# Q and K as three fp32r products each, narrower probability transposes, and a convolution loop written out

## What is computed

```
# convolution block: 1x1 (128 -> 64), 3x3 in 32 groups, 1x1 (64 -> 128), each with batch norm
h = relu(bn(conv(x, w1)));  h = relu(bn(conv(h, w2, groups=32)));  x = relu(bn(conv(h, w3)) + x)
# attention block, windows of 7 x 7, rolled by 3, 8 heads of 16 channels
y = layernorm(x) * norm1_w + norm1_b
q, k, v = split(windows(roll(y)) @ qkv_w.T)
attn = softmax(q @ k.T * 16**-0.5 + bias + mask)
x = x + unroll((attn @ v) @ proj_w.T + proj_b)
z = layernorm(x) * norm2_w + norm2_b
out = x + gelu(z @ fc1_w.T + fc1_b) @ fc2_w.T + fc2_b
```

## Time and profile before

| | |
|---|---|
| time, median of 3 runs | 4525.73 us (4525.11 to 4525.87) |
| time of the profiled execution | 4518.32 us |
| its span, first to last instruction | 4516.2 us |
| busy share of the span: PE, DVE, ACT, POOL | 98%, 70%, 76%, 49% |
| matmul instructions | 71190 |

### The profile page before, as it was taken

The page is one execution under the profiler, slowest core; times in us unless marked ns, Lnnn a source line. Parts: engine busy times, 40 slices in busy tenths (PEclk is TensorE's granted clock), DMA queues, the critical chain, the costliest instruction groups (busy, mean ns, idle before and its releaser), DMA issues.

```text
span 4516.2 us, 192181 instructions
## 1 busy us (share of the span) xinstructions
PE 4423.1 (98%) x71190; PEld 3178.5 (70%) x71190; DVE 3178.4 (70%) x7717; ACT 3415.4 (76%) x5644; POOL 2207.9 (49%) x3242
## 2 busy tenths in 40 slices
PE   8999996999999999999999999999999999999998
PEld 5666665677777777777777777777777777777775
DVE  4444444777777777777777777777777777777775
ACT  3444443888888888888888888888888888888886
POOL 4444442455554545455555555455555545455553
PEclk9999998999999999999999999999999999999999
DMA  4545442011111111111111111111111111111110
GB/s 138 153 151 163 151 153 66 25 30 29 29 29 30 30 29 29 29 30 29 29 29 30 30 29 29 29 30 29 29 29 29 29 29 29 30 30 29 29 29 26
DMA packets 298330, 218.64 MB, mean 48 GB/s; under 512 B 43377, under 2 KB 245518, under 8 KB 298190
## 3 DMA queue, kind: packets, MB, share of 16 engines
q1 hardware_dynamic: 294632, 215.41, 16.4%
q10 hardware_dynamic: 3558, 1.07, 0.1%
HBM read 110.73 MB, written 111.94 MB: 49 GB/s over the span
## 4 chain that ended last, share of the span: by engine, by line
PE 97%; DVE 1%; issue 1%; ACT 0%; POOL 0%; DMA 0%; DVEq 0%; POOLq 0%; ACTq 0%
PE bank L666 16%; PE bank L608 10%; PE bank L585 8%; PE bank L509 6%; PE bank L576 6%; PE bank L641 6%; PE bank L657 6%; PE bank L595 6%; PE bank L567 5%; PE bank L620 5%; PE bank L522 5%; PE bank L631 4%; PE bank L659 4%; PE bank L658 4%; PE bank L673 2%; PE bank L487 2%
## 5 line engine op out<-in xcount | busy, mean ns | idle before, releaser
L1234 POOL TENSOR_TENSOR sc<-sc,mx 128x784 f32<-128x784 f32 x512 | 779.2, 1522 | 940.9 <-DVE mx L1068 940.9
L666 PE MATMUL bank<-g,fc_sb 128*128 128x392 f32 x2048 | 785.4, 506 | 0.1
L1221 POOL TENSOR_TENSOR res<-x,projb 98x512 f32<-98x512 f32 x256 | 326.3, 1275 | 804.2 <-DVE x L1104 804.2
L861 ACT ACTIVATE g<-bank,fc1b 128x392 f32<-128x392 f32 x1024 | 560.6, 592 | 172.6 <-PE bank L659 172.6
L1087 DVE SCALAR_TENSOR_TENSOR xn<-x,lnp 98x128 f32<-98x128 f32 x1024 | 292.8, 349 | 491.1 <-POOL lnp L1157 491.1
L608 PEld LDWEIGHTS bank<-ident_sb,sc 128*113 128x113 f32 x4096 | 495.6, 177 | 113.1 <-DVE shared L1038 109.8
L666 PEld LDWEIGHTS bank<-g,fc_sb 128*128 128x128 f32 x2048 | 348.7, 190 | 306.2 <-issue 163.1
L608 PE MATMUL bank<-ident_sb,sc 128*113 128x128 f32 x4096 | 547.8, 277 | 0.1
L1062 DVE TENSOR_TENSOR sc<-bank,shared 128x392 f32<-128x392 f32 x1024 | 528.7, 560 | 2.8 <-PE bank L595 2.8
L1068 DVE TENSOR_REDUCE mx<-sc 128x16 f32<-128x784 f32 x512 | 496.6, 970 | 18.5
L1157 POOL TENSOR_TENSOR lnp<-lnp,half 98x8 f32<-98x8 f32 x518 | 467.7, 924 | 20.3
(11 more groups left out here) (105 smaller groups left out, 8258.3 us busy)
## 6 DMA issues: line engine op xcount, KB each, us to landing
x<-x_scratch SPq DMA_DIRECT2D x768, 49.0 KB
out_x<-y SPq DMA_DIRECT2D x672, 49.0 KB
xc_even<-in_x SPq DMA_DIRECT2D x128, 196.0 KB
shared<-in_x SPq DMA_DIRECT2D x128, 196.0 KB
x_scratch<-xc_even SPq DMA_DIRECT2D x128, 196.0 KB
x_scratch<-shared SPq DMA_DIRECT2D x128, 196.0 KB
x<-x_scratch SPq DMA_DIRECT2D x256, 38.5 KB
out_x<-y SPq DMA_DIRECT2D x224, 38.5 KB
```

The costliest lines, as they stand in the source:

```text
L666: mm = nc.tensor.matmul(RC[:, 0:ST], fc2[:, c, :], g[:, c], start=c == 0, stop=c == HC - 1)
L861: nc.scalar.activation(g[:, j], ring[:, 0:ST], ACT.Gelu, bias=fc1b[:, j:j + 1]).then_inc(out_, 1)
L1234: P.tensor_tensor(out=s_r, in0=s_r, in1=m_r.to_broadcast([128, 2 * HEADS, N]), op=ALU.subtract).then_inc(sub_done, 1)
```

## The change

1. Q and K are each computed by three fp32r products, with weights `wqk_hi`, `wqk_lo` (made once, on DVE) and input `xt_hi`, `xt_lo`. `xt_hi` is made in every strip by POOL (`xt_round`: xt times one, written as fp32r), `xt_lo` by DVE (`xt_rest`: xt minus xt_hi). Values still use xt in fp32.
2. Q goes to bank 0, one of the score banks, instead of `RA`; K and Q have separate semaphores, and `RA` has two jobs a strip from the projection instead of three.
3. PE's round begins with the values, then the transposes of z, then K and Q. ACT's begins with `v_out`, `zt_out`, `k_out`, and takes `gelu` 0 and 1 ahead of the first two `pt_out`.
4. The probability transposes take 113 rows of the scores and the identity cut to 113 x 113, instead of 128 rows and 128 x 128.
5. The loop over the convolution's pairs is written out: 16 calls of `period`.
6. PE starts the convolution's first step before the last preparations of weights on DVE are done.

```diff
@@ over_pairs
-    with e.Fori(0, (BPAIRS - 2) // 2) as k:
-        period(2 * k, 0)
-        period(2 * k + 1, 1)
-    period(BPAIRS - 2, 0)
-    period(BPAIRS - 1, 1)
+    for gp in range(BPAIRS):
+        period(gp, gp % 2)
@@ PE
-                pe.wait_ge(prep, len(PREP))
+                at(pe, "fc1_scaled")
...
+            def split_product(dst, part):
+                cols = slice(C * part, C * part + C)
+                nc.tensor.matmul(dst, wqk_hi[:, cols], xt_hi[:], start=True, stop=False)
+                nc.tensor.matmul(dst, wqk_lo[:, cols], xt_hi[:], start=False, stop=False)
+                return nc.tensor.matmul(dst, wqk_hi[:, cols], xt_lo[:], start=False, stop=True)
+
+            def project_k(t):
+                pe.wait_ge(a_out, A_JOBS * t.n + 1)
+                pe.wait_ge(xt_split, t.n + 1)
+                split_product(RA[:, 0:ST], 1).then_inc(a_full, 1)
+
+            def project_q(t):
+                wait(pe, s_out, QUADS * t.n)
+                split_product(bank[0][:, 0:ST], 0).then_inc(q_full, 1)
...
-                    mm = nc.tensor.transpose(RB[j % 2][0:VT, 128 * q:128 * q + 128],
-                                             sc[:, t.u, q, j].rearrange("p h m -> p (h m)")[:, 0:VT], ident[:])
+                    mm = nc.tensor.transpose(RB[j % 2][0:VT, 128 * q:128 * q + VT],
+                                             sc[0:VT, t.u, q, j].rearrange("p h m -> p (h m)")[:, 0:VT],
+                                             ident[0:VT, 0:VT])
@@ PE, strips
-                    project(t, 0)
                     values(t, 0)
                     values(t, 1)
...
-                    project(t, 1)
+                    project_k(t)
+                    project_q(t)
@@ ACT, strips
-                    k_out(t)
                     v_out(t)
...
+                    k_out(t)
...
+                    gelu(t3, 0)
+                    gelu(t3, 1)
                 if t1.there():
                     pt_out(t1, 0)
                     pt_out(t1, 1)
                 if t3.there():
-                    gelu(t3, 0)
-                    gelu(t3, 1)
@@ DVE
+            def xt_rest(t):
+                dve.wait_ge(xt_rounded, t.n + 1)
+                V.tensor_tensor(out=xt_lo[:], in0=xt[:].rearrange("c w n -> c (w n)"), in1=xt_hi[:].bitcast(fp32),
+                                op=ALU.subtract).then_inc(xt_split, 1)
@@ DVE, strips
                     y_sum(t3)
+                if ahead.there():
+                    xt_rest(ahead)
                 if t1.there():
                     x2_out(t1)
@@ POOL
+            def xt_round(t):
+                pool.wait_ge(a_out, A_JOBS * t.n + 1)
+                wait(pool, q_full, t.n)
+                x_ = xt[:].rearrange("c w n -> c (w n)")
+                tt(xt_hi[:], x_, one[:].to_broadcast([C, ST]), ALU.mult).then_inc(xt_rounded, 1)
@@ POOL, strips
                     subtract(t)
+                if ahead.there():
+                    xt_round(ahead)
```

More of the change, by code:

```diff
@@ L141 @@
              "sign", "scaled", "exponent", "power", "signed", "tab", "tab_ps", "tab_rows", "hidden_ps", "hidden", "table_ps", "table",
-             "fc1b_ps", "fc1b", "fc1_scaled", "fc1_hi", "fc1_lo"]
+             "fc1b_ps", "fc1b", "fc1_scaled", "fc1_hi", "fc1_lo", "wqk_hi", "wqk_lo"]
 PREP = CONV_PREP + BIAS_PREP
@@ L185, in program @@
         fc1_hi, fc1_lo = [sb(f"fc1_{i}", [C, HID], fp32r) for i in ("hi", "lo")]
+        wqk_hi, wqk_lo = [sb(f"wqk_{i}", [C, 2 * C], fp32r) for i in ("hi", "lo")]
         fc2 = sb("fc2_sb", [128, HC, C])
         half = sb("half", [128, C])
+        one = sb("one", [128, 1])
         quarter = sb("quarter", [PT, 2, PAIRS])
@@ L221, in program @@
         xt = sb("xt", [C, WINS, N])
+        xt_hi, xt_lo = [sb(f"xt_{i}", [C, ST], fp32r) for i in ("hi", "lo")]
         qt = sb("qt", [C, WINS, QROWS])
@@ L241, in program @@
         RA, RB, RC = bank[4], bank[5:7], bank[7]
-        A_JOBS = 3
+        A_JOBS = 2
         SUMS, PROJECTION = 2, 3
@@ L255, in program @@
         zt_split = sem("zt_split")
+        xt_rounded, xt_split, q_full, q_sb = sem("xt_rounded"), sem("xt_split"), sem("q_full"), sem("q_sb")
         conv2_begun, vb_clear = sem("conv2_begun"), sem("vb_clear")
@@ L579, in values @@
                     mm.then_inc(b_full[0], 1)
[L581 to L586, removed]
+            def split_product(dst, part):
[4 more added lines that the diff above has]
+            def project_k(t):
+                pe.wait_ge(a_out, A_JOBS * t.n + 1)
+                pe.wait_ge(xt_split, t.n + 1)
[3 more added lines that the diff above has]
+                split_product(bank[0][:, 0:ST], 0).then_inc(q_full, 1)
             def scores(t, i):
-                pe.wait_ge(a_out, A_JOBS * t.n + 3)
+                pe.wait_ge(a_out, A_JOBS * t.n + 2)
+                pe.wait_ge(q_sb, t.n + 1)
                 wait(pe, s_out, QUADS * t.n)
@@ L893, in strips @@
                     zt_out(t3)
+                if t.there():
+                    k_out(t)
                 if t3.there():
                     nc.scalar.preload_act_table_set("gelu_and_others")
+                if t3.there():
+                    gelu(t3, 0)
+                    gelu(t3, 1)
                 if t1.there():
@@ L970, in bias_steps @@
                          op=ALU.subtract)
+                    step("wqk_hi", V.tensor_copy, wqk_hi[:], wqkv[:, 0:2 * C])
+                    step("wqk_lo", V.tensor_tensor, out=wqk_lo[:], in0=wqkv[:, 0:2 * C], in1=wqk_hi[:].bitcast(fp32),
+                         op=ALU.subtract)
             def xct_out(gp, i):
@@ L1041, in q_out @@
             def q_out(t):
-                dve.wait_ge(a_full, A_JOBS * t.n + 3)
+                dve.wait_ge(q_full, t.n + 1)
                 wait(dve, s_full, t.n)
-                V.tensor_copy(qt[:, :, 0:N], RA[:, 0:ST].rearrange("c (w n) -> c w n", n=N)).then_inc(a_out, 1)
+                V.tensor_copy(qt[:, :, 0:N], bank[0][:, 0:ST].rearrange("c (w n) -> c w n", n=N)).then_inc(q_sb, 1)
+            def xt_rest(t):
+                dve.wait_ge(xt_rounded, t.n + 1)
+                V.tensor_tensor(out=xt_lo[:], in0=xt[:].rearrange("c w n -> c (w n)"), in1=xt_hi[:].bitcast(fp32),
+                                op=ALU.subtract).then_inc(xt_split, 1)
             def zt_rest(t):
@@ L1157, in tt @@
                 return P.tensor_tensor(out=o, in0=x, in1=y_, op=op)
+            P.memset(one[:], 1.0)
             step("half", P.memset, half[:], -0.5)
```

## The result

The changed kernel takes 4702.02 us (median, 4700.11 to 4703.09), against 4525.8 us for the kernel before on the same chip: a ratio of 1.0388 (95% interval 1.0372 to 1.0403). It is slower, as forecast, but by 176 us where 66 were forecast, and above the range that ended at 4665. The profiled execution of after took 4703.09 us, 184.8 more than that of before (4518.3).

What follows compares the result with a forecast made beforehand. A cycle through PE and DVE was taken to bound the strips, +0.29 us each. Strips +72, convolution -4 and start -2 gave +66 us, 4592 on the median of 4525.7; range 4538 to 4665.

Steps and rivals of the forecast that it cites:

- What bounds the kernel: In each strip, a cycle through PE (10.01 us) and DVE up to `v_out` (4.51 us), 14.52 us in all.
- 0.5 to 0.9 forecast: Sign expected in each strip: PE idle 0.5 to 0.9 us before the first transposes, released by DVE's copy of the values.
- the fp32r products: K and Q on PE: 0.14 to 0.3 us a strip saved, but in the part where PE waits for DVE, worth 0.
- `xt_round` on POOL: In each strip, 0.76 to 0.98 us on idle POOL, inside the 1.10 us left before `xt_rest`: 0 added.
- Rival 2: POOL is late: xt_hi takes over 1.05 us and DVE waits 0.3 us more a strip; +75 us, 4667; chance 0.13.
- `xt_rest`, +0.52: The subtraction for xt_lo, in the middle of DVE's chain: 0.52 us added a strip, bounds 0.48 and 0.57.
- Transposes and the vanished wait: PE's part of a strip: 0.15 us less from 113 by 113 transposes, 0.08 less because `hidden` no longer waits.
- Convolution, -4: Writing out the convolution's loop: 4 us less in all, ends -29 and +4, with straight code stalling 1.2 us a step.
- The start's -2: At the kernel's start, PE's first convolution matmul no longer waits 2.46 us for `fc1_lo` on DVE: 2 us less.

Runs made afterwards that it cites:

- e1: The changed kernel with xt_hi written once ahead of the strips, so POOL rounds nothing per strip; `xt_rest` and all matmuls stay: 4550.6 us.
- e2: The changed kernel with xt_hi made by a second activation on ACT behind `xt_out` instead of by POOL: 4552.6 us.
- e11: The kernel before plus POOL's rounding alone, into a tile that nobody reads: 4659.1 us.
- e5: The changed kernel with one more wait: POOL begins `xt_round` only when z (`x2_norm`) is done: 4690.2 us.
- e6: The changed kernel with Q and K back as one fp32 product each, without `xt_round` and `xt_rest`: 4466.4 us.
- e4: The kernel before with only the probability transposes changed, to 113 by 113: 4513.1 us.
- e3: The kernel before with only the convolution's loop written out: 4507.7 us.
- e8: e2 with DVE's copy of the values (`v_out`) moved directly behind `y_sum`: 4702.2 us.
- e10: e2 with `v_out` moved on DVE to between `x2_out` and its statistics: 4445.0 us.
- e9: e6 with `v_out` moved on DVE directly behind `y_sum`: 4573.6 us.
- e12: e6 with `v_out` moved on DVE to between `x2_out` and its statistics: 4448.2 us.

## Why the prediction was wrong in size

**What bounds the kernel: right.** The cycle of PE and DVE through `v_out` is what moved. PE waits 0.68 us in front of the first transposes for DVE's copy (0.5 to 0.9 forecast), and the fp32r products, some 0.18 us each from start to start, lie in the part where PE waits, worth 0 in after.

**`xt_round` on POOL, "That just fits: 0 added": the step that failed.** The time it takes was right, 0.97 us within 0.76 to 0.98, and `xt_rest` found it done. But I asked only whether POOL is done in time, and not what runs on DVE meanwhile. It is z, with two inputs in SBUF, and it costs +0.59 us a strip, 147.5 us in the groups' busy time (437.1 - 289.6). Three runs give about the same by other ways: 151 (e1), 149 (e2), 136 us (e11, in the kernel before). The rule of the Trainium skill told under e5 speaks against this very edit, and I had not weighed it. Rival 2 had POOL's slot as the danger too, and a time of 4667 close to the result, but by another mechanism: POOL over 1.05 us and a wait in front of `xt_rest`. There is none, so it didn't happen, and that its time comes near is luck.

The trace of the kernel before had the effect already, once, ahead of the loop. POOL, DVE, and the line's minimum, median and maximum:

```profile
749.53 1.26 POOL L1221 TENSOR_TENSOR res<-x,projb 98x512 f32<-98x512 f32 x1
749.60 2.13 DVE L1087 SCALAR_TENSOR_TENSOR xn<-x,lnp 98x128 f32<-98x128 f32 x4 [3.73 <-POOL lnp L1157]
```
```profile
L1087 DVE SCALAR_TENSOR_TENSOR xn<-x,lnp x1024: 339/347/1340, 749.6 to 4449.4; 98x128 f32<-98x128 f32 x171
```

Four xn take 1.13 us elsewhere. Had I asked why one of 1024 took 1340 ns, the price of POOL beside such an instruction would have been on the table.

**`xt_rest`, +0.52: too dear.** Its own 0.48 was within the bounds. But between `y_sum` and its successor 0.72 us became 0.60, so +0.36 net; e2 over e6, 0.34 a strip, says the same. Why the slot behind y_sum is shorter with another instruction in it was not studied.

**Transposes and the vanished wait, -0.15 and -0.08: half.** The first eight went from 0.95 to 0.81 us, the second eight from 0.87 to 0.79; that is -0.22, and 99 ns each lies between my 96 and 104. PE's part as a whole became only 0.12 shorter. Most of the difference is at its end: over the strips of the loop, `attend` starts 0.18 us earlier behind the first transposes (8.77 us, 8.95 before), but `ot_out` starts 0.07 later behind `attend`'s last matmul (0.41 and 0.34). In e4 it is 0.03 later. Why DVE takes up `ot_out` later there, no run shows.

**Convolution, -4: too small a gain.** It was 12 us in the trace of after and 15 in that of e3, some 19 in e3's runs. The start's -2 was right: PE's first L510 came at 45.69, before at 47.60. The stalls in straight code are real, and I was right that the loop's stall is not all gain; but three steps are no sample: mean 0.6 us a step, not 1.2. With 0.6 my own sum gives it: an iteration loses 4.1 us in the loop and 4 x 0.6 = 2.4 written out, so 1.7 are gained, seven times 12. The rule of the Trainium skill (Runtime: NRT & Kernel Launch, section Instruction fetch mechanics), by which the cost lies in the jumps, gave the same -12, but by luck. Its claim that fetch is mostly hidden elsewhere is not borne out: straight code loses 2.4 us in four steps. The loop happens to lose as much beside its idle 1.7, so the two cancel.

With its terms as measured (z, `xt_rest`, the rest of DVE's part, PE's part), the prediction's own sum would be +0.59 + 0.36 - 0.04 - 0.12 = +0.79 a strip, and 198 - 12 - 2 = +184 us.

## What to carry to other kernels

Before work goes to an idle POOL, list what DVE runs in that window: a DVE instruction with two SBUF inputs that started behind POOL's ended only behind it in every pair looked at, and the profile books that time as busy. Look for it in the minimum, median and maximum of one line, not in the waits. And a copy or a helper moved up in an in-order queue pays only from the moment its input exists; e8 and e10 differ by two places of one copy and by 257 us, e9 and e12 by one place and by 125.

## What the runs showed of the hardware

- z takes 346 ns as a rule and up to 935 beside a POOL instruction that reads SBUF; xt_lo 0.55 and 1.61 us. A factor column of one number per partition, spread over the row, is enough of a second SBUF input. A copy from PSUM, batch statistics, and sums with one PSUM input are not slowed by POOL (y in e5; statistics, 277 ns, and copy, 665 ns, beside `residual1` and the factors in every strip of after). ACT's exponential on SBUF (0.86 us) beside z lengthens neither.
- POOL's own multiplication of 128x392 takes 0.84 us alone, and beside z up to 1.00: longer by what is left of the z that runs when it starts.
- A transpose in fp32 takes 109 ns in the form 128 by 128 and 99 in the form 113 by 113; an fp32r product of 392 columns 0.18 us, an fp32 one 0.69.
- Code without jumps loses 0 to 2.4 us in a run of 288 matmuls of the convolution (7.94 to 10.29 us in after), 0.6 us a step on average, in gaps of which all but one of 17 end 1.2 to 1.6 us after a 16 KiB packet of instructions has landed.
